# Three node stages of a graph-network kernel on one Trainium2 core: written out over three buffers, normalised in part by ScalarE, the next addition placed ahead of the wait for the root

## Chip, cores and metric

The kernel runs on one core of one Trainium2 chip. The metric is the device time of the whole program in microseconds (us). Before the change it is 16785.31 us, the median of three runs.

## What is computed

Four residual graph layers over 12500 nodes with 128 features each, and 212500 edges in the order of their target node:

```python
x = _layernorm(x + _L0_gnn_ref(...), axis=-1)
x = _layernorm(x + _L1_gnn_ref(...), axis=-1)
x = _layernorm(x + _L2_gnn_ref(x, edge_index, edge_attr_128, W, b, gamma, beta), axis=-1)
x = _layernorm(x + _L3_gnn_ref(x, edge_index_t, kernel, kernel_attention), axis=-1)

def _layernorm(x, axis=-1, eps=1e-05):
    m = jnp.mean(x, axis=axis, keepdims=True)
    v = jnp.var(x, axis=axis, keepdims=True)
    return (x - m) / jnp.sqrt(v + eps)
```

L0 is a weighted neighbour sum with two branches, L1 two rounds of neighbour sum and MLP with batch norm, L2 a message MLP on gathered source and target rows, L3 an attention layer (exp of a clipped score, its sum as denominator). The change touches only what stands between the layers: the addition of a layer's result to x, the layer norm, and the projection of the new x that the next layer gathers.

## The kernel before

The program is one instruction stream per engine, with semaphores written by hand. Long edge passes, in which GpSimd (POOL) issues one indirect DMA for 128 gathered or scattered rows at a time, alternate with short **node stages**. The last three of them are `node_*(n2, 2)`, `node_*(n3, 3)` and `node_*(n4, 4)`, after L1, L2 and L3; here they are called stages 2, 3 and 4. An edge pass begins only when the stage before it has stored its last table, and a stage begins only when the pass before it has added its last tile.

A stage walks over the nodes in 14 steps (`NSTEPS`) of 7 blocks (`BSTEP`) of 128 nodes. In step s:

- SyncE (SP) loads the old x of the step into `xin`, and later stores the new x from `xnew` and, in stages 2 and 3, the projected table from `tabrow`. `xin` and `xnew` have two buffers each. All three transfers stand in SP's one queue in program order, each behind its waits.
- TensorE (PE), in stage 2 alone, first turns the layer's result (`y_all`, features on partitions) into `y_bank` (line 1308, here the **y transposes**), which VectorE adds. In stages 2 and 3 it transposes `xnew` (1303, 1287), and multiplies the transposed block, once ScalarE has copied it to `proj_t`, with weights (1318 and 1320 in stage 2, 1294 in stage 3).
- VectorE (DVE) adds (1836, 1839; in stage 4 1842 to 1846 with a division by the attention's sum), takes bn_stats of each block (1849), forms mean and variance in `mean_var` (1542 to 1548), waits for the root, takes the reciprocal (1853) and scales all seven blocks (1855).
- ScalarE (ACT) takes the root (926), copies the transposed block out of PSUM (951, 931; here the **copy to proj_t**), and evacuates the product (958 and 959 in stage 2, 936 to 938 in stage 3).

In stage 2 the projection lags two steps: in turn s PE does the transposes of block s-2, then the y transposes of step s, then the matmuls of s-2. ACT's turn s in stage 2 is: copy to `proj_t` of s-2, root of s, evacuation of s-2. Every engine works strictly through its own program, so such an order decides who waits for whom. PE is written out in stage 2; the other engines' loops run two steps per lap (`run_steps`).

The first node stage (FirstNodeSems, lines 880 to 912 on ACT and 1785 to 1820 on DVE) is not changed. It is written out already, and there ScalarE does one of two normalisations with `ACT.Identity`, scale and bias per partition (887).

Of the kernel before, what the change touches and what calls it, by code (L numbers as in the profile page):

```python
# [14 lines left out]
ALU = mybir.AluOpType  # L15
# [109 lines left out]
class NodeSems:  # L125


    def __init__(self, own, nth, steps):
        self.own, self.done, self.half = own, nth * steps, nth * (steps // 2) * 16
        self.var, self.std, self.ch, self.xnew = own["var"], own["std"], own["ch"], own["xnew"]  # L130
        self.xl, self.st, self.tab = ([own[f"{what}{k}"] for k in range(2)] for what in ("xl", "st", "tab"))
        self.ptr, self.ptrc, self.pmm, self.pev = own["ptr"], own["ptrc"], own["pmm"], own["pev"]
        self.tr, self.one = own["tr"], own["one"]
# [52 lines left out]
def gnn_program(nc, t, out):  # L186
# [38 lines left out]
    with ctx:  # L225
# [208 lines left out]
        xin = take((2, BSTEP, D))  # L434
        xnew = take((2, BSTEP, D))
        tabrow = take((2, BSTEP * HROW))
        stats = take((BSTEP, 6))
        mom = [take((BSTEP,)) for _ in range(8)]
        proj_t = take((2, BSTEP * D))
        take = carver(work, 0)  # L440
# [52 lines left out]
        nodes = {k: sem(f"node_{k}") for k in ("var", "std", "ch", "xnew", "xl0", "xl1", "st0", "st1", "tab0", "tab1",  # L493
                                               "ptr", "ptrc", "pmm", "pev", "tr", "one")}
        n2, n3, n4 = (NodeSems(nodes, nth, NSTEPS) for nth in range(3))
# [99 lines left out]
        def node_sp(sp, n, table, to, kind):  # L595
# [4 lines left out]
            else:  # L600
                before = {3: n2, 4: n3}[kind]
                for k in range(2):
                    sp.wait_ge(before.st[k], before.half + NSTEPS // 2 * 16)
                    sp.wait_ge(before.tab[k], before.half + NSTEPS // 2 * 16)
# [4 lines left out]
            def step(s, k, u):  # L609
                if live(s, NSTEPS):  # L610

                    wait(sp, n.xnew, s + (n.done - 1))
                    sp.dma_start(xin[:, k], blocks_of(table, s)).then_inc(n.xl[k], 16)
                g, (kk, _) = s - 2, back(k, u, 2, 2)
                if live(g, NSTEPS):
                    sp.wait_ge(n.xnew, g + (n.done + 1))
                    if kind == 4 and isinstance(g, int) and g == NSTEPS - 1:
# [7 lines left out]
                g, (kk, _) = s - 3, back(k, u, 3, 2)  # L625
                if kind != 4 and live(g, NSTEPS):
                    sp.wait_ge(n.pev, g + (n.done + 1))
# [5 lines left out]
            run_steps(sp, NSTEPS, 2, 3, step)  # L633
# [3 lines left out]
        def _(sp):  # L637
# [83 lines left out]
            for k in range(2):  # L721
                sp.wait_ge(n3.tab[k], n3.half + NSTEPS // 2 * 16)
                sp.wait_ge(n3.st[k], n3.half + NSTEPS // 2 * 16)
            edge_in(p4, False)
            node_sp(sp, n4, x3_tab, out, 4)
            for k in range(2):
                sp.wait_ge(n4.st[k], n4.half + (NSTEPS // 2 + (k == 1)) * 16)
# [119 lines left out]
        def _(act):  # L847
# [75 lines left out]
            def node_act(n, kind):  # L923
                def root(s):
                    act.wait_ge(n.var, s + (n.done + 1))
                    act.activation(mom[6], mom[5], ACT.Sqrt).then_inc(n.std, 1)

                def evacuate(g, kk, gu):

                    act.wait_ge(n.ptr, g + (n.done + 1))  # L930
                    act.activation(proj_t[:, kk], bank_slot(kk)[:, 0:BSTEP * D], ACT.Copy).then_inc(n.ptrc, 1)
                    wait(act, n.tab[kk], gu * 16 + n.half)
                    act.wait_ge(n.pmm, g + (n.done + 1))
                    res = bank_slot(kk)[:, 0:BSTEP * 2 * D].rearrange("p (b f) -> p b f", f=2 * D)
                    row = tabrow[:, kk].rearrange("p (b f) -> p b f", f=HROW)
                    act.activation(row[:, :, 0:D], res[:, :, 0:D], ACT.Copy)
                    act.activation(row[:, :, D + 1:D + 2], res[:, :, D:D + 1], ACT.Copy)
# [1167 lines left out]
```

## Time and profile before

| quantity | value |
|---|---|
| median of the runs | 16785.31 us |
| lowest and highest of three | 16775.68 and 16787.63 us |
| span of the profiled execution (first to last instruction) | 14549.9 us |
| own time of the profiled execution | not given apart from its span; the median is 2235.4 us above the span |
| busy share of the span: POOL, DVE, PE, ACT | 70%, 45%, 39%, 14% |
| stage 2 | 9746 to about 9858 us |
| stage 3 | 12099 to about 12207 us |
| stage 4 | 14438 to 14550 us |

The span leaves out what lies ahead of the first and behind the last instruction. A stage's position is given in us from the start of the span. The granted clock of PE is given as a share of 2.4 GHz: 0.5 is the lower level (1.2 GHz), 1.0 the upper one.

### The profile page before, as it was taken

How to read it: one execution, taken by the hardware profiler on the slowest of the kernel's cores; microseconds unless marked ns; L12 is line 12 of the kernel's file. 1: busy time of each engine (PE TensorE's matmuls, PEld its weight loads, DVE VectorE, ACT ScalarE, POOL GpSimd, SP SyncE). 2: the span in 40 equal slices, each digit the busy share in tenths (PEclk: the TensorE clock that was granted, in tenths of full speed). 3: DMA queues.
4: the chain of work that ended last, by engine and by line, in shares of the span. 5: the costliest groups of instructions: out<-in, count | busy, mean ns of one | idle time of the engine just before them, and what ended most of it. 6: DMA issues, size and time to landing. Idle time of an engine off the chain costs nothing.

```text
span 14549.9 us, 185642 instructions
## 1 busy us (share of the span) xinstructions
PE 5642.2 (39%) x42509; PEld 4641.8 (32%) x42510; DVE 6490.2 (45%) x25163; ACT 2071.4 (14%) x8809; POOL 10118.0 (70%) x10603
## 2 busy tenths in 40 slices
PE   7200002546655111111441111127888885444443
PEld 2000002333334100000441111127888884444442
DVE  9201113667765100000541111137888886656666
ACT  0000000000002111111010000015666662000000
POOL 4777777777774677777237777746777774777775
PEclk9655555768765555555555555559999996555555
DMA  4444449211112212211321111125555554333333
GB/s 109 127 126 140 127 141 81 53 50 52 52 51 61 54 46 46 46 46 44 92 52 20 20 20 20 20 51 132 131 131 131 131 130 113 80 80 79 80 80 86
DMA packets 1400883, 1138.59 MB, mean 78 GB/s; under 512 B 445673, under 2 KB 1261295, under 8 KB 1400143
## 3 DMA queue, kind: packets, MB, share of 16 engines
q1 hardware_dynamic: 1049493, 567.59, 16.8%
q0 software_dynamic: 335264, 554.74, 15.6%
q10 hardware_dynamic: 15778, 12.82, 0.3%
q14 instruction: 276, 2.26, 0.1%
q8 instruction: 72, 1.18, 0.0%
HBM read 871.76 MB, written 262.57 MB: 78 GB/s over the span
## 4 chain that ended last, share of the span: by engine, by line
POOL 58%; issue 19%; DVE 4%; PE 2%; DMA 1%; ACT 1%; DVEq 0%; SPq 0%; POOLq 0%; ACTq 0%
POOL work L807 34%; POOL rows_b L822 12%; POOL work L834 11%; DVE work L1887 2%; DMA x_tab<-work 0%; DVE work L1849 0%; DVE work L1855 0%; PE ps L1261 0%; DVE work L1801 0%; PE ps L1357 0%; PE ps L1224 0%; PE ps L1229 0%; DVE work L1941 0%; PE ps L1218 0%; DVE big L1632 0%
## 5 line engine op out<-in xcount | busy, mean ns | idle before, releaser
L807 POOL DMA_INDIRECT work<-q_tab,pay_a x1760 | 1673.5, 951 | 715.8 <-issue 535.1
L807 POOL DMA_INDIRECT work<-h_tab,pay_a x1760 | 1671.8, 950 | 673.5 <-issue 536.1
L807 POOL DMA_INDIRECT work<-in_x_dram,pay_a x1760 | 1709.4, 971 | 545.2 <-issue 536.0
L822 POOL DMA_INDIRECT rows_b<-work,big x1760 | 1706.7, 970 | 540.0 <-issue 536.2
L834 POOL DMA_INDIRECT work<-z_tab,work x1760 | 1662.8, 945 | 539.2 <-issue 536.0
L775 POOL DMA_INDIRECT edges_a<-work x1660 | 1607.4, 968 | 567.0 <-issue 508.7
L1625 DVE TENSOR_TENSOR big<-big,ps 128x128 f32 (+1 forms) x5280 | 1494.7, 283 | 940.8 <-PE ps L1127 531.9
L1868 DVE TENSOR_SCALAR work<-work,iota_p 128x512 bf16<-128x512 bf16 (+1 forms) x1320 | 560.3, 425 | 2220.0 <-PE ps L1240 1946.5
L1431 PE MATMUL ps<-work 128*128 128x129 f32 x3520 | 916.9, 441 | 1220.5 <-DVE work L1617 1220.5
L1127 PE MATMUL ps<-work 128*128 128x128 f32 x3520 | 749.3, 379 | 1376.2 <-DMA work<-in_x_dram,pay_a 995.5
L1431 PEld LDWEIGHTS ps<-work 128*128 128x128 f32 x3520 | 788.2, 329 | 1256.5 <-DVE big L1625 1162.3
L1958 DVE TENSOR_SCALAR work<-iota_h,lo_chunk 128x128 bf16<-128x128 bf16 x1760 | 329.3, 270 | 1862.9 <-PE ps L1276 1858.1
L1617 DVE TENSOR_SCALAR work<-iota,work 128x128 f32<-128x128 f32 x3520 | 1134.8, 364 | 16.2
L1127 PEld LDWEIGHTS ps<-work 128*128 128x128 f32 x3520 | 639.3, 272 | 1561.9 <-issue 1495.5
L1276 PE MATMUL ps<-work 128*128 128x32 bf16 x5280 | 284.3, 194 | 1916.2 <-DMA work<-z_tab,work 1879.9
L1240 PE MATMUL ps<-big,work 128*128 x1760 | 292.0, 259 | 1878.7 <-ACT work L913 1864.6
L1276 PEld LDWEIGHTS ps<-work 128*128 128x128 bf16 x5280 | 238.2, 108 | 1962.4 <-issue 1957.7
L1393 PE MATMUL ps<-wc,work 128*128 128x128 f32 x3520 | 715.5, 285 | 355.8 <-ACT work L1010 187.1
L1240 PEld LDWEIGHTS ps<-big,work 128*128 128x128 bf16 x1760 | 183.3, 104 | 1987.4 <-issue 1946.7
L1394 PE MATMUL ps<-work,ident 128*128 128x128 f32 x3520 | 681.8, 275 | 0.0
L1395 PE MATMUL ps<-big,work 128*128 x3520 | 681.8, 275 | 0.0
L1393 PEld LDWEIGHTS ps<-wc,work 128*128 128x128 f32 x3520 | 533.1, 191 | 448.9 <-issue 223.6
(346 smaller groups left out, 12240.8 us busy)
## 6 DMA issues: line engine op xcount, KB each, us to landing
work<-lo_rows SPq DMA_DIRECT2D x1320, 128.0 KB
work<-edges_a SPq DMA_DIRECT2D x440, 256.0 KB
work<-in_edge_attr_dram SPq DMA_DIRECT2D x166, 640.0 KB, 5.1
rows_b<-work SPq DMA_DIRECT2D x80, 550.0 KB, 7.5
work<-rows_b SPq DMA_DIRECT2D x110, 400.0 KB, 3.2
work<-in_x_dram,pay_a POOLq DMA_INDIRECT x1760
rows_b<-work,big POOLq DMA_INDIRECT x1760
work<-z_tab,work POOLq DMA_INDIRECT x1760
```

The costliest lines, as they stand in the source:

```text
L775: pool.indirect_dma_start(out=edges_a, out_offset=bass.IndirectOffsetOnAxis(ap=stage_pos[:, k, j:j + 1], axis=0), in_=stage_a[:, k, j, :], ...
L807: pool.indirect_dma_start(out=ring[:, at:at + width], out_offset=None, in_=table, in_offset=bass.IndirectOffsetOnAxis(ap=pay[:, e, 1:2], a ...
L822: pool.indirect_dma_start(out=rows_b, out_offset=bass.IndirectOffsetOnAxis(ap=pos_b[:, s * G + j:s * G + j + 1], axis=0), in_=message[:, k ...
L834: pool.indirect_dma_start(out=rows_h[:, at:at + H3], out_offset=None, in_=z_tab, in_offset=bass.IndirectOffsetOnAxis(ap=pay_b_i[:, e, 1:2] ...
L1127: m = pe.matmul(ps[:, kk % 4, j * D:(j + 1) * D], lhsT=onehot[:, kk % 4, j], rhs=rows[:, at:at + D], start=True, stop=True)
L1393: pe.matmul(o, lhsT=attr_t[:, kk % 2, j * P:(j + 1) * P], rhs=wc[:, 2, :], start=True, stop=False)
L1394: pe.matmul(o, lhsT=ident[:, :], rhs=rows[:, at:at + D], start=False, stop=False)
L1395: m = pe.matmul(o, lhsT=onehot_t[:, kk % 2, j * P:(j + 1) * P], rhs=p_all[:, bass.ds(bl[j] * D, D)], start=False, stop=True)
L1431: m = pe.matmul(ps[:, sums + j // 2, (j % 2) * 256:(j % 2) * 256 + D + 1], lhsT=onehot[:, kk % 4, j], rhs=rows[:, at:at + D + 1], start=Tr ...
L1617: ins = dve.tensor_scalar(onehot[:, k % 4, j], iota[:, :], pst[:, k, j, 0:1], scale, ALU.is_equal, ALU.mult)
L1625: dve.tensor_tensor(o, o, tile_sums, ALU.add).then_inc(p.acc, 1)
L1868: dve.tensor_scalar(turned, lo_bc[:, k % 4], iota_p[:, 0:1], None, ALU.is_equal).then_inc(p.oht, 1)
```

## The change

All three stages are written out (no loop), with three buffers for `xin` and `xnew` and two sets of `mom` and `stats`. The seven blocks are scaled by ScalarE, but for the first 3 (stage 2) or 2 (stage 3) that VectorE keeps (`SHARE`); ScalarE does all seven in stage 4. The epsilon moves into ScalarE's root as a bias, and `mean_var` becomes five operations. VectorE issues the addition of step s+1 between the variance of s and the reciprocal of s. ScalarE's turn becomes: root of s, copy to `proj_t`, scaling of s, evacuation. In stage 4 the product with the reciprocal sum and the addition become one operation for each block. SP's load of step s waits for the addition of s-3, the store lags three steps, and the table four.

```diff
+        xin = take((3, BSTEP, D))
+        xnew = take((3, BSTEP, D))
+        SHARE = {2: 3, 3: 2, 4: 0}
...
+            for s in range(NSTEPS + 4):
+                if s < NSTEPS:
+                    wait(sp, n.add, n.done + s - 2)
+                    sp.dma_start(xin[:, s % 3], blocks_of(table, s)).then_inc(n.xl[s % 3], 16)
+                g, kk = s - 3, (s - 3) % 3
+                if 0 <= g < NSTEPS:
+                    sp.wait_ge(n.xnew, n.done + g + 1)
...
+                g, kk = s - 4, s % 2
+                if kind != 4 and 0 <= g < NSTEPS:
+                    sp.wait_ge(n.pev, n.done + g + 1)
...
             def node_act(n, kind):
-                def tables(s, k, u):
-                    g, (kk, gu) = s - 2, back(k, u, 2, 2)
-                    if live(g, NSTEPS):
-                        act.wait_ge(n.ptr, g + (n.done + 1))
-                        act.activation(proj_t[:, kk], turned_bank, ACT.Copy).then_inc(n.ptrc, 1)
-                    if live(s, NSTEPS):
-                        root(s)
...
+                lag = {2: 2, 3: 1, 4: 1}[kind]
+                for s in range(NSTEPS + (lag if kind != 4 else 0)):
+                    g = s - lag
+                    tabled = kind != 4 and 0 <= g < NSTEPS
+                    if s < NSTEPS:
+                        m = mom[s % 2]
+                        act.wait_ge(n.var, n.done + s + 1)
+                        act.activation(m[6], m[5], ACT.Sqrt, bias=eps2[:, 0:1]).then_inc(n.std, 1)
+                    if tabled:
+                        act.wait_ge(n.ptr, n.done + g + 1)
+                        wait(act, n.pmm, n.done + g - 1)
+                        act.activation(proj_t[:, g % 2], turned_bank if kind == 2 else bank_slot(g % 2)[:, 0:BSTEP * D], ACT.Copy).then_inc(n.ptrc, 1)
+                    if s < NSTEPS:
+                        act.wait_ge(n.rdy, n.done + s + 1)
+                        for j in range(SHARE[kind], BSTEP):
+                            ins = act.activation(xnew[:, s % 3, j], xnew[:, s % 3, j], ACT.Identity, scale=m[7][:, j:j + 1], bias=m[4][:, j:j + 1])
+                        ins.then_inc(n.xnew, 1)
+                    if tabled:
+                        wait(act, n.tab[g % 2], g // 2 * 16 + n.half)
+                        act.wait_ge(n.pmm, n.done + g + 1)
...
             def node_pe(n, kind):
+                def tables(s):
+                    g = s - 2
+                    if 0 <= g < NSTEPS:
+                        fed(g)
+                        wait(pe, n.ptrc, n.done + g)
...
+                    if s < NSTEPS:
+                        wait(pe, n.add, n.done + s)
                         for j in range(BSTEP):
+                            m = pe.transpose(y_bank[:, j * D:(j + 1) * D], y_all[:, s * (BSTEP * P) + j * P:s * (BSTEP * P) + (j + 1) * P], ident[:, :])
                         m.then_inc(n.tr, 1)
+                    if 0 <= g < NSTEPS:
+                        pe.wait_ge(n.ptrc, n.done + g + 1)
+                        wait(pe, n.pev, n.done + g)
...
             def node_dve(n, kind):
+                def add(s):
+                    xn = xnew[:, s % 3]
+                    wait(dve, n.st[s % 3], n.slot[s % 3] + s // 3 * 16)
+                    if kind != 4:
+                        wait(dve, n.ptr, n.done + s - 2)
+                    if kind == 2:
+                        dve.wait_ge(n.tr, s + 1)
...
+                        for j in range(BSTEP):
+                            ins = dve.scalar_tensor_tensor(out=xn[:, j], in0=at[:, j, 0:D], scalar=den[:, 1, j:j + 1], in1=xin[:, s % 3, j], op0=ALU.mult, op1=ALU.add)
+                        ins.then_inc(n.add, 1)
...
+                add(0)
+                for s in range(NSTEPS):
...
+                    dve.scalar_tensor_tensor(out=m[5], in0=m[2], scalar=1.0 / D, in1=m[3], op0=ALU.mult, op1=ALU.add).then_inc(n.var, 1)
+                    if s + 1 < NSTEPS:
+                        add(s + 1)
+                    dve.wait_ge(n.std, n.done + s + 1)
+                    c(dve.reciprocal(m[7], m[6]))
+                    dve.scalar_tensor_tensor(out=m[4], in0=m[0], scalar=-0.5, in1=m[7], op0=ALU.mult, op1=ALU.mult).then_inc(n.rdy, 1)
+                    if SHARE[kind]:
+                        dve.wait_ge(n.rdy, n.done + s + 1)
+                        for j in range(SHARE[kind]):
+                            ins = dve.tensor_scalar(xn[:, j], xn[:, j], m[7][:, j:j + 1], m[4][:, j:j + 1], ALU.mult, ALU.add)
+                        ins.then_inc(n.xdve, 1)
```

How the change moves instructions in stage 2 is shown on three engines. First ScalarE before, from the roots of steps 0 and 1 to the evacuation of block 1 (926 is the root, 951 the copy to `proj_t`, 958 and 959 the evacuation):

```order
L926 ACTIVATE work<-work 128x7 [waits node_var] x2
L951 ACTIVATE work<-ps 128x896 [waits node_ptr]
L926 ACTIVATE work<-work 128x7 [waits node_var]
L958 ACTIVATE big<-ps 128x896 [waits node_pmm]
L959 ACTIVATE work<-ps 128x896
L951 ACTIVATE work<-ps 128x896 [waits node_ptr]
L926 ACTIVATE work<-work 128x7 [waits node_var]
L958 ACTIVATE big<-ps 128x896 [waits node_pmm]
L959 ACTIVATE work<-ps 128x896
```

The same engine after, turns 2 and 3 (942 is the root, 946 the copy to `proj_t`, 950 the scaling, 957 and 958 the evacuation):

```order
L942 ACTIVATE work<-work,eps2 128x7 [waits node_var]
L946 ACTIVATE work<-ps 128x896 [waits node_ptr]
L950 ACTIVATE work<-work 128x128 [waits node_rdy]
L950 ACTIVATE work<-work 128x128 x3
L957 ACTIVATE big<-ps 128x896 [waits node_pmm]
L958 ACTIVATE work<-ps 128x896
L942 ACTIVATE work<-work,eps2 128x7 [waits node_var]
L946 ACTIVATE work<-ps 128x896 [waits node_ptr]
```

The copy to `proj_t` stood ahead of the root of its turn and now stands behind it, and four scalings stand between it and the evacuation.

VectorE after, the end of one step and the start of the next in stage 2 (1865 and 1866 end the variance, 1839 is the addition, 1870 and 1871 make scale and bias, 1875 is the scaling, 1859 bn_stats):

```order
L1865 SCALAR_TENSOR_TENSOR work<-work 128x7 [waits node_ch]
L1866 SCALAR_TENSOR_TENSOR work<-work 128x7 [waits node_ch]
L1839 TENSOR_TENSOR work<-ps,work 128x896 [waits node_tr,n0_xl0,node_ptr,n0_st0]
L1870 RECIPROCAL work<-work 128x7 [waits node_std]
L1871 SCALAR_TENSOR_TENSOR work<-work 128x7 [waits node_ch]
L1875 TENSOR_SCALAR work<-work 128x128 [waits node_rdy]
L1875 TENSOR_SCALAR work<-work 128x128 x2
L1859 BN_STATS work<-work 128x6 [waits node_add]
```

The addition, with its wait for the y transposes (node_tr), came after the scaling of the step before; it now comes ahead of that step's reciprocal.

TensorE after, from the matmuls of one block to the waits of the next in stage 2 (1304 transposes `xnew`, 1309 are the y transposes, 1319 and 1321 the matmuls):

```order
L1319 MATMUL ps<-bias,ones_h 128x128
L1321 MATMUL ps<-wc,work 128x256
L1304 MATMUL ps<-ident,work 128x128 [waits node_ptrc,node_xdve,node_xnew]
L1304 MATMUL ps<-ident,work 128x128 x6
L1309 MATMUL ps<-ident,big 128x128 [waits node_add]
L1309 MATMUL ps<-ident,big 128x128 x6
L1319 MATMUL ps<-bias,ones_h 128x2x128 [waits node_pev,node_ptrc]
```

TensorE's order in stage 2 is what it was: the y transposes of a step stand behind the matmuls of three blocks earlier.

## Rows read from the trace of the kernel before

**Rows 1.** The page: span, and shares of the chain that ended last.

```profile
span 14549.9 us, 185642 instructions
POOL 58%; issue 19%; DVE 4%; PE 2%; DMA 1%; ACT 1%; DVEq 0%; SPq 0%; POOLq 0%; ACTq 0%
```

**Rows 2.** Windows, stages 2, 3, 4: length, PE, PEld, DVE, ACT, POOL busy, PE clock, DMA share, GB/s.

```profile
9746.00:9860.00 114.00, 77.93 (x450) 63.31 (x451) 75.84 (x322) 38.34 (x56) 0.00 (x0) 0.90 0.62 174
12099.00:12207.00 108.00, 54.47 (x294) 50.17 (x294) 78.55 (x329) 30.44 (x71) 0.00 (x0) 0.71 0.66 184
14438.00:14550.00 112.00, 0.00 (x0) 0.00 (x0) 95.94 (x366) 2.91 (x14) 0.00 (x0) 0.50 0.40 115
```

**Rows 3.** The lines of the three additions: ns min/median/max, first and last start us.

```profile
L1836 DVE TENSOR_TENSOR work<-ps,work x14: 1078/1091/1092, 9750.1 to 9836.1; 128x896 f32<-128x896 f32 x14
...
L1839 DVE TENSOR_TENSOR work<-big,work x14: 1081/1092/1093, 12103.3 to 12185.9; 128x896 f32<-128x896 f32 x14
...
L1846 DVE TENSOR_TENSOR work<-work x14: 1091/1091/1093, 14442.9 to 14540.5; 128x896 f32<-128x896 f32 x14
```

**Rows 4.** Timeline, DVE, one step of stage 2: start, us, operation, [idle before <-releaser].

```profile
9767.75 1.08 DVE L1836 TENSOR_TENSOR work<-ps,work 128x896 f32<-128x896 f32 x1
9768.87 1.45 DVE L1849 BATCH_NORM_STATS2 work<-work 128x6 f32<-128x128 f32 x7
...
9771.07 0.17 DVE L1548 TENSOR_TENSOR work<-work 128x7 f32<-128x7 f32 x1
...
9771.75 1.89 DVE L1855 TENSOR_SCALAR work<-work 128x128 f32<-128x128 f32 x7
```

**Rows 5.** Timeline, ACT, the same step of stage 2.

```profile
9771.27 0.21 ACT L926 ACTIVATE work<-work 128x7 f32<-128x7 f32 x1 [3.12 <-DVE work L1548]
9771.88 0.92 ACT L958 ACTIVATE big<-ps 128x896 f32<-128x896 f32 x1 [0.40 <-PE ps L1320]
...
9773.49 0.93 ACT L951 ACTIVATE work<-ps 128x896 f32<-128x896 f32 x1
```

**Rows 6.** Timeline, PE, stage 2: first and last group at the upper level; transposes at the lower.

```profile
9756.03 1.75 PE L1303 MATMUL ps<-ident,work 128*128 128x128 f32 x7 [3.04 <-DVE work L1855]
...
9768.20 0.28 PE L1318 MATMUL ps<-bias,ones_h 128*128 128x256 bf16 x1 [1.10 <-ACT work L951]
...
9772.45 0.93 PE L1308 MATMUL ps<-ident,big 128*128 128x128 f32 x7
```

**Rows 7.** Timeline, ACT, first node stage: seven scalings.

```profile
4662.50 2.80 ACT L887 ACTIVATE work<-work 128x128 f32<-128x128 f32 x7 [1.40 <-DVE work L1806]
```

**Rows 8.** Timeline, PE, two steps of stage 3.

```profile
12125.66 3.39 PE L1294 MATMUL ps<-kaug,work 128*128 128x130 f32 x14 [3.41 <-ACT work L931]
12128.85 0.96 PE L1287 MATMUL ps<-ident,work 128*128 128x128 f32 x7
12133.68 3.40 PE L1294 MATMUL ps<-kaug,work 128*128 128x130 f32 x14 [3.87 <-ACT work L931]
12136.88 1.70 PE L1287 MATMUL ps<-ident,work 128*128 128x128 f32 x7
```

**Rows 9.** Timeline, the end of stage 2: last variance; the chain: last table store.

```profile
9839.44 0.17 DVE L1548 TENSOR_TENSOR work<-work 128x7 f32<-128x7 f32 x1
...
9854.42 3.20 DMA q_tab<-work
```

**Rows 10.** Waits in stage 3: who waited for whom, us in total, times, longest.

```profile
DVE work L1839 <- DMA x_tab<-work: 6.2, 7, 2.1
```

**Rows 11.** Timeline, PE, stage 3: the matmuls at the upper level.

```profile
12139.58 1.83 PE L1294 MATMUL ps<-kaug,work 128*128 128x130 f32 x14 [1.01 <-ACT work L931]
```

**Rows 12.** Timeline, DVE, stage 4: the small operation ahead of a division; scalar_tensor_tensor of the pass before.

```profile
14456.09 0.17 DVE L1842 TENSOR_SCALAR work<-big 128x7 f32 x1
...
12093.14 0.60 DVE L1990 SCALAR_TENSOR_TENSOR work<-beta,spread,work 128x128 f32<-128x128 f32 x2
```

**Rows 13.** DMA issues of stage 4: count, KB each, median us from issue to landing.

```profile
out_dram<-work SPq DMA_DIRECT2D x13, 448.0 KB, 4.7
```

More of the change, by code:

```diff
@@ L125, with __init__ @@
 class NodeSems:
-    def __init__(self, own, nth, steps):
+    def __init__(self, own, first, nth, steps):
         self.own, self.done, self.half = own, nth * steps, nth * (steps // 2) * 16
         self.var, self.std, self.ch, self.xnew = own["var"], own["std"], own["ch"], own["xnew"]
-        self.xl, self.st, self.tab = ([own[f"{what}{k}"] for k in range(2)] for what in ("xl", "st", "tab"))
+        self.add, self.rdy, self.xdve = own["add"], own["rdy"], own["xdve"]
+        self.xl, self.st = first.xl, first.st
+        self.tab = [own[f"tab{k}"] for k in range(2)]
+        self.laps = [(steps - k + 2) // 3 * 16 for k in range(3)]
+        self.slot = [(nth + 1) * n for n in self.laps]
+        self.stored = [(nth + 2) * n for n in self.laps]
         self.ptr, self.ptrc, self.pmm, self.pev = own["ptr"], own["ptrc"], own["pmm"], own["pev"]
@@ L601, in node_sp @@
                 before = {3: n2, 4: n3}[kind]
+                for k in range(3):
+                    sp.wait_ge(before.st[k], before.stored[k])
                 for k in range(2):
-                    sp.wait_ge(before.st[k], before.half + NSTEPS // 2 * 16)
                     sp.wait_ge(before.tab[k], before.half + NSTEPS // 2 * 16)
@@ L923, in node_act @@
             def node_act(n, kind):
[L924 to L928, printed above, removed]
-                    act.wait_ge(n.ptr, g + (n.done + 1))
[L931 to L937, printed above, removed]
-                    act.activation(a_all[:, bass.ds(g * BSTEP, BSTEP)], res[:, :, D + 1:D + 2].rearrange("p b o -> p (b o)"), ACT.Copy).then_inc(n.pev, 1)
@@ L1820, in _ @@
             dve.wait_ge(n0.xnew, NSTEPS)
+            chain = Chain(dve, n2.ch)
             def node_dve(n, kind):
-                c = Chain(dve, n.ch)
-                def step(s, k, u):
-                    c.begin(s * COUNT + CHAIN0)
-                    xn = xnew[:, k]
-                    wait(dve, n.st[k], u * 16 + n.half)
+                c = chain
+                def add(s):
+                    xn = xnew[:, s % 3]
+                    wait(dve, n.st[s % 3], n.slot[s % 3] + s // 3 * 16)
@@ L1848, in step @@
-                    for j in range(BSTEP):
-                        ins = dve.bn_stats(stats[:, j, :], xn[:, j])
-                    c(ins)
-                    mean_var(c, stats, mom, 1e-5).then_inc(n.var, 1)
-                    dve.wait_ge(n.std, s + (n.done + 1))
-                    c(dve.reciprocal(mom[7], mom[6]))
-                    for j in range(BSTEP):
-                        ins = dve.tensor_scalar(xn[:, j], xn[:, j], mom[4][:, j:j + 1], mom[7][:, j:j + 1], ALU.subtract, ALU.mult)
@@ L1968, in _ @@
             dve.wait_ge(n2.pev, n2.done + NSTEPS)
+            for k in range(3):
+                dve.wait_ge(n2.st[k], n2.stored[k])
             for k in range(2):
-                dve.wait_ge(n2.st[k], n2.half + NSTEPS // 2 * 16)
                 dve.wait_ge(n2.tab[k], n2.half + NSTEPS // 2 * 16)
@@ L2028, in _ @@
             dve.wait_ge(n3.pev, n3.done + NSTEPS)
+            for k in range(3):
+                dve.wait_ge(n3.st[k], n3.stored[k])
             for k in range(2):
-                dve.wait_ge(n3.st[k], n3.half + NSTEPS // 2 * 16)
                 dve.wait_ge(n3.tab[k], n3.half + NSTEPS // 2 * 16)
```

145 lines of the change are left out of this document (61 added, 84 removed).

## Prediction

> **What bounds the kernel now.** I read the page first. Its chain is POOL for 58% [rows 1]: the edge passes are bound by GpSimd's indirect DMAs, and the change does not touch them. A node stage stands between two passes that wait for its ends, so every us that a stage gains or loses is a us of the program, until its own end. The windows come next. The three stages last 114, 108 and 112 us with their edges, POOL is not busy in any, and DVE is busy 67%, 73% and 86% [rows 2]. The lines of the additions give the pace, (last start minus first) over 13: stage 2 takes (9836.1 - 9750.1)/13 = 6.62 us a step, stage 3 82.6/13 = 6.35, stage 4 97.6/13 = 7.51 [rows 3]. What ends last in a step differs between the stages:
>
> - Stage 4 has no projection. One DVE chain fills the step.
> - Stage 3 is the DVE chain plus 6.2 us in seven waits for a store that frees one of two buffers [rows 10].
> - Stage 2 has two loops of almost one length. DVE needs 5.9 us (from 9767.75 to the end of the scaling, 9771.75 + 1.89 [rows 4]). The other loop runs through PE and ACT: the matmuls begin at 9768.20 [rows 6], the evacuation behind them at 9771.88, the copy to proj_t at 9773.49 and takes 0.93 [rows 5]. So the next matmuls can begin at 9774.45, a loop of 6.3 us. The matmuls alone are 3.65 of it.
>
> **The change, part by part.** I cost each stage by the loop that binds it afterwards.
>
> **Stage 4: gains.** On DVE a step then holds: two small operations for the denominator, 0.17 us each [rows 12] and 0.2 to 0.25 with the wait between them, together 0.45; seven scalar_tensor_tensor at the spacing of the pair of L1990, 0.60 - 0.34 = 0.26, so 1.9; bn_stats to the next start 1.5; the variance, which before ended 2.37 us after the start of bn_stats (9771.24 - 9768.87) [rows 4], with one waited operation fewer, so 0.7; the reciprocal and the bias 0.4. That is 4.95. ACT needs 2.8 for seven scalings [rows 7] and a root of 0.21 [rows 5], about 3.0, beside DVE. The third buffer has to come round too: addition 2.4, rest of the step before 0.4, bn_stats and variance 2.2, next addition 2.4, reciprocal 0.4, scaling 2.8, store 4.7 [rows 13], in all 15.3 for three steps, or 5.1. I take 5.0. 13 x (7.51 - 5.0) = 32.6 less; the first division now waits for the load (0.9 more) and the last scaling is 2.8 instead of 1.89 (0.9 more) [rows 4, 7]. **-31 us**. Bounds: 4.9 and 5.5 a step, so -32 and -24.
>
> **Stage 3: gains less.** DVE falls to addition 1.1, bn_stats and variance 2.2, reciprocal and bias 0.4, two scalings 0.6: 4.3. ACT has root 0.1, copy 0.9, five scalings 2.0, evacuation 1.1: 4.2. The DMA queue is nearer: the stage moves three transfers of 448 KB [rows 13], 1.38 MB, a step, and at 184 GB/s the engines were 0.66 busy [rows 2], so full use is 279 GB/s and 5.0 us a step. On PE the transposes, the copy, and the matmuls follow each other. At the upper clock that is 0.93 + 1.0 + 1.83 [rows 8, 11]; at the lower one 1.70 + 1.0 + 3.40 = 6.1 [rows 8]. The granted clock was 0.71 of the upper [rows 2]. I take 5.2, just above the DMA's floor: 13 x 1.15 = **-15 us**. Bounds: 5.0 and 6.3, so -18 and -1.
>
> **Stage 2: loses.** Here two moves meet. DVE now issues the addition of s+1 ahead of the reciprocal of s. That addition needs the y transposes of s+1, which PE's program has behind the matmuls of block s-2. Those need the copy to proj_t of s-2, and ACT now issues that copy behind the root of s, which waits for the variance of s. Nothing of this was a loop before: the copy stood ahead of the root, and the addition behind the scaling, so PE ran ahead while DVE worked. Now it is one chain round four engines, once a step from step 2 on, in which nothing overlaps:
>
> - variance of s to root, root to copy: 0.15; copy 0.93 [rows 5]; to PE 0.05
> - X: matmuls of s-2, transposes of s-1, y transposes of s+1. At the upper level they ran from 9768.20 to 9773.38, X = 5.2 [rows 6]. At the lower level everything takes twice that (seven transposes 1.75 instead of 0.93): 10.4 [rows 6]
> - to DVE, addition 1.15; reciprocal and bias 0.45 [rows 4]
> - ACT: four scalings, 1.55 to the next start, from seven in 2.80 [rows 7]; the two evacuations 1.6 (9771.88 to 9773.49) [rows 5]. DVE's way to the variance of s+1, three scalings 0.85 and 2.2, is about as long: 3.1
>
> Without X this is 5.9 us. In those 5.9 us PE stands idle in one piece. What PE's clock does then is seen in stage 3: after 3.4 us of idling the matmuls took 3.39, the lower level, and the transposes behind them 0.96, the upper one; after 3.87 us both were at the lower level, for 4.9 us [rows 8]. So low for 3.2 to 4.9 us, which adds half of that to X: 6.8 to 7.65. The idling is longer here, so I take 7.6 and a step of 13.5.
>
> The Trainium skill says this of the clock (TensorE: Matmul & The Clock Gate, "HAM oscillation"): a loop whose bursts are separated by long waits starts each burst throttled, every single time. The trace agrees for the two steps shown in stage 3 [rows 8]; were a burst throttled to its end, X would be 10.4.
>
> Of the 13 periods the first two stay near 5.9, since no block is projected yet; the eleven others were (86.0 - 11.8)/11 = 6.75. 11 x (13.5 - 6.75) = +74. The end of the stage grows too. Before, the last variance was at 9839.6 and the last table store at 9854.4, 14.8 us [rows 9], because block 11 had its matmuls behind it. After, three blocks are left: copy, matmuls, evacuation is 0.95 + 3.65 + 1.6 = 6.2 each, 18.6 at the upper level and some 2 more at a mixed one, so +6. **+80 us**. Bounds: X = 5.2 gives 11 x 4.35 + 4 = +52, X = 10.4 gives 11 x 9.55 + 8 = +113. The longer step makes every load and store of stage 2 early, so they cost nothing.
>
> **What costs nothing.** The loops' branches and register instructions went beside other work in stages 2 and 3 and are inside the measured periods of stage 4. ACT has a second queue's worth of work but no DMA behind it. SP waits behind xnew and the evacuation, as before; its load of s+1 goes out about two steps ahead. The next pass's first gather waits only for the last table store, which is in the sum. The clock at the head of the next pass does not matter while POOL bounds it.
>
> **Sum.** +80 - 15 - 31 = +34 us. The profiled execution's own time is not known apart from its span, 2235 us under the median, so I add to the median and take what lies around the span as unchanged: 16785 + 34 = **16819 us**. The span would go from 14550 to about 14584.
>
> **The rivals.** About 0.2% (34 us) is what a measurement can tell from no change; my sum lies on it.
>
> 1. *PE low throughout the burst.* Stage 2 costs +113: +67, 16852. For it: 5.9 us of idling, more than any in stage 3. Against: the 0.96 us transposes [rows 8]. 13%.
> 2. *PE stays at the upper level.* Stage 2 costs +52: +6, 16791, no difference. For it: clock 0.90 in stage 2 before [rows 2]. Against: there PE idled 1.1 us ahead of the matmuls [rows 6], here 5.9. 10%.
> 3. *Faster: the ring does not close.* If the y transposes of s+1 were done before the variance of s, stage 2 would keep its PE and ACT loop of 6.3 plus a root, so near 0, and the sum would be -46: 16739. It decides at one point, whether PE's queue reaches the y transposes before the copy of s-2. For it: DVE, ACT and PE have 4.4 to 5.3 us of work a step, so there is room. Against: PE issued matmuls, transposes and y transposes in this order without exception [rows 6]. That would also be the case in which the change does what it says. 9%.
> 4. *Stages 3 and 4 give little.* A saturated queue makes stores land late and the third buffer still waits, 6.2 and 6.0 us a step: -2 and -18, so +60, 16845. For it: waits for stores in stage 3 [rows 10]. Against: in stage 4 the DMA was 0.40 busy [rows 2]. 6%.
>
> **How the numbers follow.** My case has 62%, and its time lies evenly about the limit: 31% over it and 31% under. Slower by over 0.2%: 31 + 13 + 6 = 0.50. Within: 31 + 10 = 0.41. Faster: 0.09. The range leaves out rival 3 and little else: its low end takes X = 5.2 with the best of the two gains, +52 - 18 - 32 = +2, and 5 us for the spread of the three runs; its high end takes X = 10.4 with the poor gains, +113 - 1 - 24 = +88, less a little since the three hardly meet: 16782 to 16868.
>
> **What would show it.** In stage 2 the additions (now L1839) would start 13 to 14 us apart from the third on, with DVE idle before them until PE's transposes; ACT would wait for nothing between root and copy; the clock in the stage would fall from 0.90 to about 0.7. Stage 3 should be 93 us long and stage 4 about 81. I am wrong if stage 2's period is under 8, if DVE in stage 2 waits for a DMA, or if a pass between the stages has changed its length.

## Result and profile after

The changed kernel takes 16802.97 us, the median of 20 runs, and the kernel before 16779.45 us on the same chip, also 20 runs. The ratio is 1.0014, with a 95% interval of 1.0008 to 1.0021: +23.5 us, clear of noise and within the 0.2% that the prediction calls no difference (the upper end of the interval is just over it). The forecast was 16819, range 16782 to 16868, with 0.50 on slower by over 0.2%, 0.41 on within, 0.09 on faster.

The profile was taken of an execution of 16801 us, whose span is 16799.6 us. That of the kernel before was of another kind, told under e1; what follows compares stages, and for before it uses the second trace, e1, wherever it does not name [rows] or the first trace.

The three stages of the changed kernel in the windows view (length, busy us of PE, PEld, DVE, ACT and POOL, granted clock, DMA share, GB/s), as [rows 2]:

```profile
11037.00:11233.00 196.00, 108.47 (x448) 83.20 (x448) 59.98 (x253) 60.01 (x112) 0.00 (x0) 0.73 0.35 99
14013.00:14100.00 87.00, 45.03 (x294) 39.32 (x294) 59.94 (x246) 58.05 (x141) 0.00 (x0) 0.82 0.87 230
16721.00:16799.60 78.60, 0.00 (x0) 0.00 (x0) 64.13 (x325) 42.01 (x112) 0.00 (x0) 0.50 0.59 163
```

Against the windows of [rows 2], stage 2 went from 114 to 196 us, stage 3 from 108 to 87, stage 4 from 112 to 79. ScalarE took over work in all three (60, 58 and 42 us busy against 38, 30 and 3), and VectorE shed it. The lines of the additions, as [rows 3], for stages 2, 3 and 4 (in stage 4 seven instructions a step), with the waits ahead of the one in stage 2:

```profile
L1839 DVE TENSOR_TENSOR work<-ps,work x14: 1091/1092/1093, 11041.4 to 11201.9; 128x896 f32<-128x896 f32 x14
its engine sat idle before it (us, times) until:
  PE ps L1309: 104.1, 12
...
L1842 DVE TENSOR_TENSOR work<-big,work x14: 1091/1093/1094, 14017.8 to 14078.0; 128x896 f32<-128x896 f32 x14
...
L1849 DVE SCALAR_TENSOR_TENSOR work<-big,work x98: 343/346/353, 16726.4 to 16789.1; 128x128 f32<-128x128 f32 x98
```

VectorE waited 104.1 us in 12 waits for PE's y transposes, which it did not wait for at all in the first trace of before (its 9.6 us there were for stores) and for 1.5 us in e1. The additions of stage 2 now span 160.5 us for 13 steps, where they spanned 86.0 [rows 3]. One turn of the ring in the timeline of stage 2, all three engines:

```profile
11092.36 1.09 DVE L1839 TENSOR_TENSOR work<-ps,work 128x896 f32<-128x896 f32 x1 [9.28 <-PE ps L1309]
...
11093.60 0.17 DVE L1871 SCALAR_TENSOR_TENSOR work<-work 128x7 f32<-128x7 f32 x1
11093.80 1.65 ACT L950 ACTIVATE work<-work 128x128 f32<-128x128 f32 x4 [9.47 <-DVE work L1871]
...
11095.35 0.90 ACT L957 ACTIVATE big<-ps 128x896 f32<-128x896 f32 x1
...
11096.63 0.17 DVE L1866 SCALAR_TENSOR_TENSOR work<-work 128x7 f32<-128x7 f32 x1
11096.95 0.29 ACT L942 ACTIVATE work<-work,eps 128x7 f32<-128x7 f32 x1
...
11097.14 0.90 ACT L946 ACTIVATE work<-ps 128x896 f32<-128x896 f32 x1
...
11098.09 0.39 PE L1319 MATMUL ps<-bias,ones_h 128*128 128x256 bf16 x1 [5.93 <-ACT work L946]
...
11098.28 1.91 PE L1321 MATMUL ps<-wc,work 128*128 128x256 f32 x4
...
11103.66 0.65 PE L1321 MATMUL ps<-wc,work 128*128 128x256 f32 x2
...
11104.91 0.93 PE L1309 MATMUL ps<-ident,big 128*128 128x128 f32 x7
11106.04 1.09 DVE L1839 TENSOR_TENSOR work<-ps,work 128x896 f32<-128x896 f32 x1 [9.25 <-PE ps L1309]
```

It reads as one chain: addition, bias, four scalings, evacuation, root, copy, matmuls, transposes, y transposes, addition. VectorE's way to the variance (done at 11096.80) and ScalarE's to the end of the evacuation (11097.05) are about equally long, as the prediction had it. From addition to addition it takes 13.68 us. PE idles 5.93 us ahead of the matmuls, begins them at the lower level (1.91 us for four, which take 1.03 at the upper level in e5) and ends the burst at the upper one. The granted clock says the same, in the column ahead of the last two, for the begin and the end of the burst:

```profile
11098.00:11100.00 2.00, 1.91 (x6) 1.36 (x7) 0.00 (x0) 0.04 (x1) 0.00 (x0) 0.50 0.95 241
11104.00:11106.00 2.00, 1.84 (x16) 1.52 (x14) 0.00 (x0) 0.00 (x0) 0.00 (x0) 1.00 0.03 8
```

### The profile page after: what moved, and what is told of

It reads as the page before. It is cut to its first block and busy times, and to the rows that moved or that the text cites. A ratio compares the mean times of both kernels' runs of the same rounds, so it can differ in the third digit from the quotient of the medians.

```text
span 16799.6 us, 184963 instructions
## 1 busy us (share of the span) xinstructions
PE 6291.7 (37%) x42429; PEld 4999.5 (30%) x42510; DVE 6347.3 (38%) x24967; ACT 2159.3 (13%) x9033; POOL 10290.5 (61%) x10603
## 5 line engine op out<-in xcount | busy, mean ns | idle before, releaser
L816 POOL DMA_INDIRECT work<-q_tab,pay_a x1760 | 1759.5, 1000 | 1243.4 <-remote 562.4
L784 POOL DMA_INDIRECT edges_a<-work x1660 | 1689.8, 1018 | 811.1 <-issue 534.2
L1275 PE MATMUL ps<-work 128*128 128x32 bf16 x5280 | 482.6, 192 | 2055.3 <-issue 1933.5
L1239 PE MATMUL ps<-big,work 128*128 x1760 | 365.9, 252 | 2153.8 <-issue 2059.1
L1126 PE MATMUL ps<-work 128*128 128x128 f32 x3520 | 707.7, 366 | 865.0 <-DMA work<-in_x_dram,pay_a 348.7
L1275 PEld LDWEIGHTS ps<-work 128*128 128x128 bf16 x5280 | 322.3, 107 | 2215.6 <-issue 2212.0
L1397 PE MATMUL ps<-work,ident 128*128 128x128 f32 x3520 | 780.0, 296 | 392.4 <-issue 392.4
L1396 PE MATMUL ps<-wc,work 128*128 128x128 f32 x3520 | 808.7, 298 | 197.0 <-issue 163.6
L1397 PEld LDWEIGHTS ps<-work,ident 128*128 128x128 f32 x3520 | 602.3, 205 | 490.0 <-issue 489.9
L1398 PE MATMUL ps<-big,work 128*128 x3520 | 738.1, 293 | 13.7 <-issue 12.1
```

What stands on the lines that cost most here:

```text
L784: pool.indirect_dma_start(out=edges_a, out_offset=bass.IndirectOffsetOnAxis(ap=stage_pos[:, k, j:j + 1], axis=0), in_=stage_a[:, k, j, :], ...
L816: pool.indirect_dma_start(out=ring[:, at:at + width], out_offset=None, in_=table, in_offset=bass.IndirectOffsetOnAxis(ap=pay[:, e, 1:2], a ...
L1126: m = pe.matmul(ps[:, kk % 4, j * D:(j + 1) * D], lhsT=onehot[:, kk % 4, j], rhs=rows[:, at:at + D], start=True, stop=True)
L1275: m = pe.matmul(ps_flat[:, bass.ds(bl[n * G + j] * H, H)], lhsT=onehot_h[:, k % 2 * 4 + n, j], rhs=rows_h[:, at + c * H:at + (c + 1) * H], ...
L1396: pe.matmul(o, lhsT=attr_t[:, kk % 2, j * P:(j + 1) * P], rhs=wc[:, 2, :], start=True, stop=False)
L1397: pe.matmul(o, lhsT=ident[:, :], rhs=rows[:, at:at + D], start=False, stop=False)
```

## Experiments

Stages in all the traces. Stages 2 and 3 are taken from 4 us ahead of the first addition (when the first loads go out) to VectorE's memset that opens the next pass, stage 4 from the same point to the end of the span. "Against before" is the median minus that of the kernel before on the same chip, with the ratio's interval. The chips of the sessions differ (16779, 16764, 16626 us for the kernel before), so only differences and stages are compared.

| kernel | stage 2 | additions of stage 2, 13 steps | stage 3 | stage 4 | against before |
|---|---|---|---|---|---|
| e1, before again | 117.0 | 88.9 | 108.7 | 111.1 | -1.0 (0.999 to 1.0011) |
| changed | 198.4 | 160.5 | 85.4 | 77.2 | +23.5 (1.0008 to 1.0021) |
| e2, copy ahead of root | 194.9 | 158.6 | 88.3 | 77.2 | +26.3 (1.0007 to 1.0026) |
| e3, late addition | 176.5 | 141.3 | 89.9 | 77.2 | +10.7 (0.9996 to 1.0015) |
| e4, both | 118.1 | 86.8 | 87.7 | 77.2 | -48.8 (0.996 to 0.9983) |
| e5, PE kept busy | 166.0 | 132.2 | 88.2 | 77.2 | -2.1 (0.9988 to 1.0006) |
| e6, y transposes early | 114.5 | 79.0 | 87.7 | 77.1 | -56.5 (0.9952 to 0.9978) |
| e7, e6 and one step ahead | 108.1 | 75.0 | 89.5 | 77.2 | -59.0 (0.995 to 0.9977) |
| e8, VectorE scales 4 | 195.5 | 157.5 | 88.3 | 90.0 | +36.1 (1.0011 to 1.003) |
| e9, e7 and stores sooner | 104.8 | 72.3 | 88.5 | 77.2 | -65.4 (0.9948 to 0.9975) |
| e10, late addition in 3 and 4 | 198.0 | 160.1 | 89.1 | 84.2 | +31.8 (1.0008 to 1.0029) |

**e1: the kernel before, again.** No edit.

> The kernel before, unchanged, profiled in the same session as the others. The theory that the first trace of the kernel before was of a quicker execution than the timed ones expects a span within 20 us of the time, some 16780, with the 2235 us that the first trace lacks spread over the edge passes and none of them in the node stages, whose additions start 6.6, 6.35 and 7.5 us apart as in the first trace. The rival, that the rest lies outside the span in the kernel before, expects a span of 14550 again.

The span was 16758.9 us, with a median of 16763. POOL's waits ahead of one of its lines of indirect DMAs show a part of what the first trace lacks ("remote": the profile finds no instruction that ended the wait):

```profile
POOL work L807 <- issue: 1398.9, 4546, 9.2
POOL work L807 <- remote: 1268.9, 697, 15.5
```

The first trace has 1607.2 us of the kind "issue", none over 0.3 us, and none of the kind "remote" on that line, so e1 idles some 1060 us more there by these two kinds. The edge pass after stage 2 takes 2780.8 us here (memset to first addition) and 2242.9 there, the pass after stage 3 2617.3 and 2235.9, and the first addition of stage 2 starts at 11036.0 and 9750.1 us. The additions of the stages are 6.84, 6.27 and 7.51 us apart, against 6.62, 6.35 and 7.51 [rows 3]. So the 2209 us between the two spans lie inside the span and outside the three stages: 919 in the two edge passes between them, 1286 ahead of stage 2. Around the span lie 2 us in each timed run whose span is known. The first trace told stages 3 and 4 to within 1 us, but stage 2 was 114.3 us long in it and 117.0 in e1.

**e2: the copy to proj_t ahead of the root, in stage 2.**

```diff
+                    if tabled and kind == 2:
+                        act.wait_ge(n.ptr, n.done + g + 1)
+                        wait(act, n.pmm, n.done + g - 1)
+                        act.activation(proj_t[:, g % 2], turned_bank if kind == 2 else bank_slot(g % 2)[:, 0:BSTEP * D], ACT.Copy).then_inc(n.ptrc, 1)
                     if s < NSTEPS:
                         m = mom[s % 2]
                         act.wait_ge(n.var, n.done + s + 1)
                         act.activation(m[6], m[5], ACT.Sqrt, bias=eps2[:, 0:1]).then_inc(n.std, 1)
-                    if tabled:
+                    if tabled and kind != 2:
...
```

> The changed kernel with one of the two moves undone: in stage 2 ScalarE's copy to proj_t stands ahead of the root again. The theory of the ring says that a ring remains, only shorter by the variance: bias of s ready, scaling 1.55, evacuation 1.6, copy 0.93, PE's burst X, addition 1.15, reciprocal and bias 0.45, so 5.8 us and X, a step of 13.5 again and the stage 0 to 3 us shorter than the changed kernel's 198. The rival, that the root ahead of the copy alone makes the loss, expects a step of 6.5 to 7 and a program 75 to 85 us below the changed kernel.

The line of the addition in stage 2 of e2, with the waits ahead of it:

```profile
L1843 DVE TENSOR_TENSOR work<-ps,work x14: 1091/1092/1093, 11037.6 to 11196.2; 128x896 f32<-128x896 f32 x14
its engine sat idle before it (us, times) until:
  PE ps L1313: 102.3, 12
```

The wait for PE is still 102.3 us, the steps are 13.7 us from the fourth on, and the stage is only 3.5 us shorter. That much is no effect of the edit that can be told: e8, whose stage 2 is the changed kernel's, takes 195.5 us. The root ahead of the copy is not what makes the loss by itself; the scalings and the evacuation, which wait for the late addition too, hold the copy back as well.

**e3: the addition behind the scaling, in stage 2.**

```diff
-                    if s + 1 < NSTEPS:
+                    if s + 1 < NSTEPS and kind not in (2,):
                         add(s + 1)
...
                         ins.then_inc(n.xdve, 1)
+                    if s + 1 < NSTEPS and kind in (2,):
+                        add(s + 1)
```

> The changed kernel with the other move undone: in stage 2 VectorE adds after its scaling again, the copy stays behind the root. The theory of the ring expects variance to root and copy 1.1, X, addition 1.15, bn_stats and variance 2.2: 4.6 us and X. With PE at a mixed clock (X 7.5) that is 12.1 us a step, with PE at the upper level (X 5.2) 9.8. So the program is 17 to 42 us below the changed kernel. The rival, that the addition ahead of the reciprocal alone makes the loss, expects a step of 6.5 to 7 and 75 to 85 us below.

The stage is 22 us shorter than the changed kernel's, the program 13 (10.7 against 23.5 over before), where 17 to 42 were expected; the intervals of the two totals overlap. Without the first two steps, of 4.9 us each, it is (141.3 - 9.8)/11 = 12.0 us a step, against 12.1 expected. The ring is shorter and still closed.

**e4: both orders of before, in stage 2**, with the three buffers, ScalarE's scalings and written-out code kept (the edits of e2 and e3 together).

> The changed kernel with both moves undone in stage 2, the three buffers and ScalarE's scalings kept. The theory of the ring expects that the chain now takes two steps to come round (8.3 us and X, 13.5 for two), so 6.4 to 7 us a step, the stage 80 us shorter than the changed kernel's, and the program 50 to 60 us below the kernel before. If something else in the change made stage 2 slow (ScalarE's scalings, the third buffer, code that is written out), the step stays over 9 us.

The same line and its waits in e4:

```profile
L1843 DVE TENSOR_TENSOR work<-ps,work x14: 1082/1092/1092, 11038.6 to 11125.4; 128x896 f32<-128x896 f32 x14
its engine sat idle before it (us, times) until:
  PE ps L1313: 21.8, 11
```

86.8/13 = 6.68 us a step, the stage 80 us shorter than the changed kernel's, the program 48.8 below before (50 to 60 were expected). The whole loss of stage 2 was the pair of orders. Nothing else in the change slowed it by more than the 1.1 us between this stage and e1's: one move undone gives back 3.5 us at most, the other 22, both 80.

**e5: PE kept busy in the ring.** 30 transposes are added whose result nobody reads.

```diff
+                    if 2 <= s < NSTEPS:
+                        pe.wait_ge(n.add, n.done + s + 1)
+                        for j in range(30):
+                            pe.transpose(ps[:, 5, 384:512], ident[:, :], ident[:, :])
```

> The changed kernel, with 30 transposes of a constant that nobody reads put on PE in steps 2 to 13 of stage 2, behind the addition of the step and ahead of the wait for the copy to proj_t, some 4 us of the 5.9 us in which PE idles. They are wasted work. The theory that the ring costs 5.9 us and a burst X, and that X is 7.7 instead of 5.2 because PE's clock falls in the idle time, expects X near 5.2 and a step of 11.1 to 11.4 instead of 13.7: the stage 25 to 30 us shorter than the changed kernel's 198, though PE does more. If the clock does not follow PE's work there, the step stays at 13.7 or grows by what the 30 transposes take beyond the idle time.

One turn of the ring in the timeline of e5, from one addition to the next (the added transposes are the row of 30):

```profile
11042.87 1.09 DVE L1843 TENSOR_TENSOR work<-ps,work 128x896 f32<-128x896 f32 x1 [6.69 <-PE ps L1309]
...
11044.01 3.49 PE L1314 MATMUL ps<-ident 128*128 128x128 f32 x30 [1.35 <-DVE work L1843]
...
11048.59 0.28 PE L1323 MATMUL ps<-bias,ones_h 128*128 128x256 bf16 x1 [1.08 <-ACT work L946]
...
11052.84 0.93 PE L1309 MATMUL ps<-ident,big 128*128 128x128 f32 x7
11053.97 1.09 DVE L1843 TENSOR_TENSOR work<-ps,work 128x896 f32<-128x896 f32 x1 [6.68 <-PE ps L1309]
```

A step is 11.10 us, and the burst X from 11048.59 to 11053.77 is 5.18 us, wholly at the upper level; the granted clock over the stage is 0.94, where it was 0.73. The stage is 32 us shorter (25 to 30 were expected) with 360 matmuls more. So of the ring's 13.68 us, 5.9 are the other engines, 5.2 PE's work, and 2.6 the clock.

**e6: the y transposes one step earlier on PE**, ScalarE's and VectorE's new orders kept.

```diff
-                    if s < NSTEPS:
-                        wait(pe, n.add, n.done + s)
+                    for r in ((0, 1) if s == 0 else (s + 1,)):
+                        if r < NSTEPS:
+                            wait(pe, n.add, n.done + r)
...
```

> The changed kernel with one edit in PE's order in stage 2: the y transposes of step s+1 stand ahead of the matmuls of block s-2 instead of behind them, while ScalarE's and VectorE's new orders stay. The theory of the ring expects that it now takes two steps to come round, 5.9 us and X for two, so that the loop of matmuls 3.65, evacuation 1.6, root 0.2 and copy 0.9 binds: 6.4 to 6.8 a step, the stage 78 to 84 us shorter than the changed kernel's, the program 45 to 60 us below the kernel before. If the new orders on ScalarE or VectorE were bad in themselves, the step stays over 9.

The line of the addition in stage 2 of e6, with its waits:

```profile
L1840 DVE TENSOR_TENSOR work<-ps,work x14: 1090/1092/1092, 10979.6 to 11058.6; 128x896 f32<-128x896 f32 x14
its engine sat idle before it (us, times) until:
  DMA x_tab<-work: 19.1, 9
...
  PE ps L1310: 3.7, 1
```

79.0/13 = 6.08 us a step. Without the first two steps (3.3 and 4.4 us), in which no block is projected yet, it is 6.5, inside the 6.4 to 6.8 expected. The wait for PE is down to 3.7 us, the one for stores of x is 19.1 (11.1 in e1), and the stage is 84 us shorter. The new orders were not bad in themselves: they needed PE's order to move with them.

**e7: transposes of xnew and copy to proj_t one step ahead as well.** PE's turn s is then the transposes of s-1, y transposes of s+1, matmuls of s-2.

```diff
+                    t = s - 1 if kind == 2 else g
+                    if kind != 4 and 0 <= t < NSTEPS:
+                        act.wait_ge(n.ptr, n.done + t + 1)
...
-                    g = s - 2
+                    g = s - 1
                     if 0 <= g < NSTEPS:
                         fed(g)
...
+                    g = s - 2
...
```

> e6 with the transposes of xnew and the copy to proj_t one step earlier too (block s-1 in turn s, the matmuls stay at s-2), which takes root and copy out of the loop between matmuls and evacuation. That loop is then 3.65 and 1.6, and PE's own work is 5.2 to 5.4: a step of 5.3 to 5.7, the stage 10 to 15 us shorter than in e6, the program 58 to 75 us below the kernel before. Rival: the three transfers of a step then crowd the DMA queue as in stage 3, or ScalarE's order puts a new wait there, and the step stays at 6.2 or more.

The stage is 6.4 us shorter than in e6, half of what was expected: 5.77 us a step over the additions, and 5.9 without the first two, instead of 5.3 to 5.7. VectorE waited 13.7 us for stores of x. That wait was not new (19.1 us in e6), but it was now the longest. The line of the addition in stage 2 of e7:

```profile
L1842 DVE TENSOR_TENSOR work<-ps,work x14: 1090/1091/1092, 10981.3 to 11056.3; 128x896 f32<-128x896 f32 x14
its engine sat idle before it (us, times) until:
  DMA x_tab<-work: 13.7, 9
```

**e8: VectorE scales 4 blocks in stages 3 and 4.**

```diff
-        SHARE = {2: 3, 3: 2, 4: 0}
+        SHARE = {2: 3, 3: 4, 4: 4}
```

> The changed kernel, with VectorE scaling 4 blocks in stages 3 and 4 instead of 2 and 0. If stage 4 is now bound by VectorE's own work (4.72 a step), four scalings of 0.26 and their start bring it to 5.8 to 5.9 and the stage to 92 us, 14 to 16 more. If a transfer or ScalarE bound it, it stays. Stage 3 (4.63 a step) is at 0.87 of the DMA queue: it should move by less than 4 us. Together the program is 12 to 20 us above the changed kernel, 35 to 44 above the kernel before.

Stage 4 grew by 12.8 us and its step from 4.72 to 5.86. The step is the one expected; the stage grew by less than the 14 to 16 expected, since what follows the last addition, 12.1 us before, is 11.1 with the last scaling shared. From one group of additions to the next, in the timeline of e8's stage 4 (VectorE only):

```profile
16604.54 1.93 DVE L1849 SCALAR_TENSOR_TENSOR work<-big,work 128x128 f32<-128x128 f32 x7
...
16606.82 1.11 DVE L1875 TENSOR_SCALAR work<-work 128x128 f32<-128x128 f32 x4
...
16610.40 1.93 DVE L1849 SCALAR_TENSOR_TENSOR work<-big,work 128x128 f32<-128x128 f32 x7
```

Stage 3 stayed where it is in the other kernels of the table. Stage 4 is bound by VectorE's own work, stage 3 is not.

Stage 2 of e8 is the changed kernel's code, and PE idles the same 5.93 us a turn. Yet its first bursts took 6.5, 7.1, 7.4 and 7.6 us before they came to 7.7, where the changed kernel has 7.9 and 7.8 in its first turns and then 7.7. So e8's stage is 2.9 us shorter. The length of the idling alone does not set how long the clock stays low.

**e9: e7 with the store of x in stage 2 one turn sooner** in SP's queue.

```diff
-                g, kk = s - 3, (s - 3) % 3
+                g = s - (2 if kind == 2 else 3)
+                kk = g % 3
```

> e7 with SP's store of x in stage 2 one turn earlier (lag 2 instead of 3), so that it goes out as soon as the scaling is done and no longer behind the evacuation that ScalarE does next. In e7 VectorE waited 13.7 us in 9 waits for such a store. If SP's order is what kept e7 at 5.77 a step, the step falls to 5.3 to 5.5, the stage from 108 to 102 to 105 us, the program 62 to 70 us below the kernel before. If the DMA queue's load is the reason, the store only lands as late as before and the stage stays at 107 to 109.

The waits for stores are gone from the line of the addition, the additions are 72.3/13 = 5.56 us apart (5.3 to 5.5 expected) and the stage is 104.8 us (102 to 105 expected). The line of the addition in stage 2 of e9:

```profile
L1843 DVE TENSOR_TENSOR work<-ps,work x14: 1091/1092/1093, 10973.2 to 11045.5; 128x896 f32<-128x896 f32 x14
its engine sat idle before it (us, times) until:
  PE ps L1312: 14.7, 11
```

So SP's order had held the stores, not the queue's load; the longest wait left is for PE. This is the quickest kernel of the study, 65.4 us (0.39%) below the kernel before. Its 6 and 9 us over e7 and e6 are less than the totals can tell; by the traces, stage 2 is 3 us shorter than e7's and 10 shorter than e6's.

**e10: the addition behind the scaling in stages 3 and 4**, the edit of e3 for the kinds 3 and 4.

> The changed kernel with the addition behind reciprocal and scaling again in stages 3 and 4, where it gave no ring. This undoes the cover of the wait for the root alone. In stage 4, bound by VectorE at 4.72 a step, the wait before was 0.27 to 0.28: the step should be 5.0 to 5.1 and the stage 4 to 5 us longer than 77.2. In stage 3, bound near the DMA queue, at most 3 us more. So the move is worth some 5 us where it helps and 70 to 80 us where it hurts. The rival, that the move made most of the gain of stages 3 and 4, expects 15 us or more in the two stages.

Stage 4 is 7.0 us longer than the changed kernel's, more than the 4 to 5 expected, with a step of 5.30 us instead of 4.72. VectorE idles 0.37 us for the root and not 0.28. The remaining 0.2 us lie where an operation now stands straight behind the one whose result it needs: from addition to bn_stats 1.95 us, where the addition gave way to the reciprocal after 1.84, and at the end of the variance. Stage 3 is inside the spread of the other traces. So the cover that the move gives is worth 7 us in the stage where it helps most, out of 34 that stage 4 gained.

## Why the prediction was right, and where not

**The direction and the mechanism of stage 2 held.** The prediction put the loss at the place where the copy behind the root meets the addition ahead of the reciprocal. e2 to e4 show the pair and not one of the two. It gave the ring 5.9 us outside PE's burst, and PE idled 5.93. It took X = 7.6, and a step of 13.5; X is 7.75 in the turn shown and the eleven steps are 13.7 on average. e5 shows both halves of X: 5.18 at the upper level where 5.2 was taken, and the rest from the clock. The stage was to cost 80 us, and it cost 81.4 against e1.

That the two agree so closely is in part luck. The eleven steps cost 75 us (13.70 against 6.89 in e1), where 74 was forecast. The first two, taken as unchanged, took 9.8 us instead of 13.1, 3.3 less. From the last addition to the end of the stage it is 33.9 us instead of 24.1, 9.8 more, where 6 was forecast. The two misses go against each other.

The other signs of the prediction: VectorE waited for a DMA in stage 2 only once, for the first load (4.0 us); ScalarE waited for nothing between root and copy; stage 3 was 85 us long instead of 93 and stage 4 77 instead of 81. No pass changed its length: in e2 to e4, on e1's chip, the pass after stage 2 took 2780.5 to 2782.3 us and the one after stage 3 2617.2 to 2624.3, where e1 has 2780.8 and 2617.3. The changed kernel's own trace is 16.5 us longer than e1's outside the stages, but from a chip on which the kernel before is 15 us slower too.

**Rival 1 and rival 2**, the burst low or high throughout, are both refuted by the timeline of stage 2, whose first matmuls are at the lower and whose last at the upper level. The clock was 0.73 in the window, with about 0.7 forecast. **Rival 3**, that the ring does not close, is refuted by the 104.1 us of waits. It is what e6 makes true, with 6.5 us a step against the prediction's 6.3 and a root. **Rival 4**, little gain in stages 3 and 4, is refuted: 23 and 34 us. A part of its mechanism is there in stage 3, where VectorE still waited for stores (6.2 us in seven waits before [rows 10]):

```profile
DVE work L1842 <- DMA x_tab<-work: 4.9, 7, 1.2
```

**The terms that were too small are stages 3 and 4.** Stage 3 was put at 5.2 us a step and -15 us "just above the DMA's floor". It took 60.2/13 = 4.63 in the changed kernel and 4.81 to 4.97 in the seven other kernels with the same stage 3; the stage is 19 to 23 us shorter than e1's. The queue was near its limit as forecast (19.9 MB at 230 GB/s is the 87 us of its window, at a DMA share of 0.87). But the first three additions came 3.3, 4.1 and 4.1 us apart, ahead of the queue, and only the ten others kept the forecast pace: 4.9 us on average in the changed kernel, 5.1 to 5.3 in the seven. The prediction applied the floor of 5.0 to all thirteen. That the three buffers are what lets the first ones run ahead was not tried by itself.

Stage 4 was put at 5.0 a step and took 4.72, a gain of 34 instead of 31. One step of VectorE in the timeline of the changed kernel:

```profile
16749.78 1.93 DVE L1849 SCALAR_TENSOR_TENSOR work<-big,work 128x128 f32<-128x128 f32 x7
...
16751.94 1.45 DVE L1859 BATCH_NORM_STATS2 work<-work 128x6 f32<-128x128 f32 x7
...
16754.06 0.16 DVE L1845 TENSOR_SCALAR work<-big 128x7 f32<-128x7 f32 x1
...
16754.50 1.93 DVE L1849 SCALAR_TENSOR_TENSOR work<-big,work 128x128 f32<-128x128 f32 x7
```

The term that was too large is VectorE's own work, 4.95 us in the prediction. The addition and the reciprocal with the bias took 2.16 (2.3 forecast), bn_stats and variance 2.12 (2.2), the denominators 0.44 (0.45). The way of the third buffer was put at 5.1 with a store of 4.7 us, but VectorE waited for no store in stage 4, and the stores landed in a median of 3.3 us. What made them land sooner was not tried. The DMA issues of stage 4 of the changed kernel (count, KB each, median us from issue to landing), loads of x and then stores:

```profile
work<-x_tab SPq DMA_DIRECT2D x14, 448.0 KB, 4.5
out_dram<-work SPq DMA_DIRECT2D x13, 448.0 KB, 3.3
```

So the third buffer never held stage 4, and VectorE's own work did, which e8 shows.

**The sum.** By the traces, changed against e1: +81.4 - 23.3 - 33.9 = +24.2, and +23.5 was measured. Forecast +80 - 15 - 31 = +34. Eleven us in the terms of stages 3 and 4, less one in stage 2, moved the result from the limit of 0.2% to inside it, so the likelier of the two classes, at 0.50, was not the one that came; the prediction said that its sum lay on that limit. That what lies around the span is unchanged was a needless assumption: nearly nothing lies there (e1).

## What to carry to other kernels

A wait moved forward to cover another one is only free if what it waits for does not stand, on its own engine, behind something that the mover releases later. Follow the order of each engine once round, and count how many steps the ring takes: here one place in PE's order made it 13.7 us a step or 6.5. A small cover (7 us in stage 4) can cost ten times that where the ring closes, and the cure is to move the producer too, and then to look at SP's order.

## What was not expected of the hardware

The profile of the kernel before that the prediction had was of an execution with a span 2209 us shorter than e1's, and with none of the "remote" waits of POOL's indirect DMAs (1268.9 us in 697 waits of up to 15.5 us in e1, 1266.1 us in 690 in the changed kernel). All the other traces and every timed run were of the longer kind. What makes POOL wait there was not tried and stays open.

A wasted burst of 30 transposes in an idle gap made the ring 2.6 us a step quicker (e5): the burst behind it ran at the upper level from its first matmul on. The Trainium skill (TensorE: Matmul & The Clock Gate, "HAM oscillation") describes bursts that each begin throttled after a long wait, and the traces of the changed kernel agree, with the first four matmuls after 5.93 us of idling in 1.91 us and the seven y transposes at the end of the burst in 0.93, what they take in e5 too.
